# Masked graph attention on one core: the four products of a row tile with rounded weights come first, and the wait for the low weights stands at the two that read them

## The chip, the cores and the metric

The kernel runs on one core of a Trainium2 chip. The metric is the device time of one execution in microseconds (us), and smaller is better. A core has five engines that run their own instruction streams and meet at semaphores: TensorE (PE in the profile; its weight loads are shown apart, as PEld), VectorE (DVE), ScalarE (ACT), GpSimd (POOL) and SyncE (SP, which here only issues DMAs).

## What is computed

With N = 8192 rows and D = 256 columns:

```python
h = jnp.maximum(_layernorm(x, axis=-1), 0.0)
h1 = h @ a[:d]
h2 = h @ a[d:]
e = jax.nn.leaky_relu(h1 + h2.T, negative_slope=0.01)
attention = jnp.where(adj > 0, e, NEG_BIG)
attention = jax.nn.softmax(attention, axis=1)
x = x + attention @ h
```

`adj` is an 8192 x 8192 matrix of int32, 256 MB, so nearly all of the memory traffic is this one matrix.

## The kernel before, in words

The exponential of the leaky sum of two scalars is a maximum of two products, so a weight is `max(r[row], g[col]) * mask` up to factors that depend on the row or on the column alone. The column's factor is put into `h`, and the row's cancels between numerator and denominator. VectorE makes the unnormalised weights with one instruction for each 128 x 512 tile (line 710: `W`).

TensorE multiplies fp32 values in a format with a shorter mantissa. To keep the precision, both factors are split: ScalarE rounds `W` to `w_hi` (line 509), VectorE subtracts to get the rest `w_lo` (line 720), and `h` is kept as `h_hi` and `h_lo` in the same way. A product is then the sum of three: `w_hi` with `h_hi` (line 869), `w_hi` with `h_lo` (line 871) and `w_lo` with `h_hi` (line 872). Columns D and D+1 of `h_hi` carry the split denominator weights.

The matrix is cut into 16 x 16 blocks of 512 x 512. A visit takes a block of 512 rows over some blocks of columns and accumulates in PSUM (`acc`, one bank for each of four row tiles t). There are 24 short visits, of four blocks of columns each, in which `h` of the remaining rows is also made beside the products (phases "whole", "early", "late"), and then eight times a short visit and a long one of twelve blocks of columns (`finals`), after which rows are finished. When a visit ends, ScalarE copies `acc` to SBUF (line 528), GpSimd adds what earlier visits of these rows stored (line 381), and VectorE makes the reciprocal of the denominators (lines 732 to 738) in the middle of its work for the next visit.

A block is worked in two pairs of column tiles (u = 0 and 1). There are 512 pairs in all, numbered g. For a pair TensorE issues 24 matmuls: for each of four row tiles t and for both u, the three products, each with its own weight load. After the first pair of each block it also transposes the mask of a later block (line 831, four instructions; they wait for `mask`, made by ScalarE on line 500, and for `W` of line 710, whose input they replace).

The order around the change is written out by hand. In the loop VectorE does for step g first the rest `w_lo` of pair g-2, then side work, then `W` of pair g. `w_hi` has four buffers (HL = 4), `w_lo` has two (LL = 2), `W` has two. The rest of pair g needs `w_hi` of that pair and waits until TensorE has used pair g-2 (line 719). On TensorE both waits of a pair, for `w_hi` (line 859, semaphore `s_hi`) and for `w_lo` (line 860, semaphore `s_lo`), stand ahead of all of its 24 matmuls. Line 863 waits inside the pair, ahead of each row tile, until the tile's bank has been copied out; it stands in the first pair of a visit only. The signal that a pair is used (line 876) comes from its last matmul.

Of the kernel before, what the change touches and what calls it, by code (L numbers as in the profile page):

```python
# [9 lines left out]
def masked_graph_attention(nc, x, adj, a, out):  # L10
# [4 lines left out]
    ds = bass.ds  # L15

    P = 128
    N, D = x.shape
    G = 4
    BLK = P * G  # L20
# [5 lines left out]
    WC = D + 2  # L26
# [26 lines left out]
    with ctx:  # L53
        def sb(name, shape, dt):
            return ctx.enter_context(nc.sbuf_tensor(name, shape, dt))
# [4 lines left out]
        def sem(name):  # L60
            return ctx.enter_context(nc.semaphore(name))

        h_hi = sb("h_hi", [P, NT, WC], f32r)
# [78 lines left out]
        s_lo = sem("lo_ready")  # L142
# [677 lines left out]
        @block.tensor  # L820
        def _(pe):
            pe.wait_ge(s_const, 1)

            def transpose_mask(n, kc, wait):

                g = n * CI + kc
                pe.wait_ge(s_mask, g + 1)
                if wait:
                    pe.wait_ge(s_w, 2 * (g - 1))
                for t in range(G):  # L830
                    last = nc.tensor.transpose(T[:, kc, t * P:(t + 1) * P], mask_words[:, kc, t, :], ident[:])  # L831
                last.then_inc(s_T, 1)

            def lay_out_first_r():

                pe.wait_ge(s_ex, 1)
                cells = r_first.rearrange("p (q e) -> p e q", e=G)
                for e in range(G):
                    last = nc.tensor.transpose(cells[:, e, :], r_all[:, e:e + 1].to_broadcast([P, P]), ident[:])
                last.then_inc(s_lay, 1)  # L840

            def sum_h(c, parity):

                h = h_bufs[parity]
                pe.wait_ge(s_z, G * (c + 1))
                for e in range(G):
                    last = nc.tensor.matmul(hs_acc, ones[:], h[:, e, :], start=c == 0 and e == 0,
                                            stop=False, skip_group_check=True)
                last.then_inc(s_hsum, 1)

            def add_row_sums():

                pe.wait_ge(s_hs, G * (NB - Q) + 1)
                nc.tensor.matmul(hs_acc, ones[:], hsum[:], start=False, stop=True,
                                 skip_group_check=True).then_inc(s_hm, 1)

            def products(V, c, g, k, start, stop):

                pe.wait_ge(s_hi, g + 1)
                pe.wait_ge(s_lo, g + 1)  # L860
                for t in range(G):
                    if start and not V.head:
                        pe.wait_ge(s_free, G * (V.v - 1) + t + 1)
                    for u in range(2):
                        tile = G * c + 2 * (k % 2) + u
                        cols = slice(u * BLK + t * P, u * BLK + (t + 1) * P)
                        rhs_hi = h_hi[:, ds(tile, 1), :].rearrange("p o w -> p (o w)")
                        rhs_lo = h_lo[:, ds(tile, 1), :].rearrange("p o w -> p (o w)")
                        nc.tensor.matmul(acc[:, t, 0:WC], w_hi[:, k % HL, cols], rhs_hi,  # L869
                                         start=start and u == 0, stop=False)  # L870
                        nc.tensor.matmul(acc[:, t, 0:D], w_hi[:, k % HL, cols], rhs_lo, start=False, stop=False)  # L871
                        last = nc.tensor.matmul(acc[:, t, 0:WC], w_lo[:, k % LL, cols], rhs_hi,  # L872
                                                start=False, stop=stop and u == 1)
                    if stop and t < G - 1:
                        last.then_inc(s_acc, 1)
                last.then_inc(s_used, 1)

            def steps(V, n, c, first, second, last):
                if V.head and first:
                    transpose_mask(0, 0, False)  # L880
                    lay_out_first_r()
                    sum_h(0, 0)
                if first and not V.head and V.its == 2:
                    pe.wait_ge(s_hl, V.c0 + Q)
                for k in range(PI):
                    kc = k // 2
                    m = c + kc
                    if V.head and m == 0 and k == 0:
                        pe.wait_ge(s_l0, 2)
                    elif V.head:  # L890
                        pe.wait_ge(s_hl, m + 1)
                    products(V, c + kc, n * PI + k, k, first and k == 0, last and k == PI - 1)
                    if k % 2 == 0 and V.head:
                        transpose_mask((m + 1) // CI, (m + 1) % CI, m > 0)
                    elif k % 2 == 0 and not (V.tail and last):
                        transpose_mask(n + 1, kc, True)
                    if V.head and k % 2 == 1 and m + 1 < Q:
                        sum_h(m + 1, (m + 1) % CI)
                    if V.head and k % 2 == 1 and m + 1 == Q:
                        transpose_mask(n + 1, 1, True)  # L900
            run(pe, steps, h_made=add_row_sums)
# [23 lines left out]
```

## Time and profile before

| | |
|---|---|
| median of 3 runs | 1642.61 us (1642.26 to 1643.2) |
| time of the profiled execution | 1641.76 us |
| its span | 1640.0 us |
| PE busy | 1600.4 us, 98% |
| PEld busy | 1589.2 us, 97% |
| DVE busy | 1431.7 us, 87% |
| ACT busy | 1182.1 us, 72% |
| POOL busy | 397.8 us, 24% |
| granted TensorE clock | 1.00 of full speed in all but the last stretch |
| DMA | 330.97 MB, 202 GB/s on average |

The busy time of an engine says how full it is, and not what it costs: an engine that is 98% busy sets the time in the stretches in which it never stands still, and in the others something else does. So the page is read for which engine is full, the waits for where the full one stands idle, and the timeline of such a place for what came last.

### The profile page before, as it was taken

The page shows a single profiled execution, that of the slowest core. Times are in us where ns is not written, and L with a number is a line of the kernel's source. Part 1 is how long each engine was busy: PE and PEld are TensorE (multiplying, and loading weights), DVE is VectorE, ACT ScalarE, POOL GpSimd, SP SyncE. Part 2 cuts the span into 40 slices and gives each one's busy share as a digit, 9 for nine tenths or more (in the row PEclk, how much of TensorE's full clock was granted, in tenths as well). Part 3 has the DMA queues.
Part 4 walks back from the last instruction along what each step waited for, and adds up shares of the span by engine and source line. Part 5 has one row for each costly group of instructions (what it writes and reads, how often), then busy time and mean ns, then how long its engine had stood idle before and what let it go on. Part 6 is the DMA issues. An engine that isn't in the chain of part 4 may idle for free.

```text
span 1640.0 us, 38962 instructions
## 1 busy us (share of the span) xinstructions
PE 1600.4 (98%) x13350; PEld 1589.2 (97%) x13350; DVE 1431.7 (87%) x2008; ACT 1182.1 (72%) x1240; POOL 397.8 (24%) x487
## 2 busy tenths in 40 slices
PE   5999999999999999999999999999999999999998
PEld 4999999999999999999999999999999999999998
DVE  7899999999999988888788888888888888888887
ACT  7788778777778766767767767767767766767763
POOL 6344224453344311201201201201301300300400
PEclk9999999999999999999999999999999999999999
DMA  6666767877777777657666656666756756666662
GB/s 206 217 204 217 229 209 223 245 221 245 244 225 232 232 210 229 198 169 206 198 185 194 210 166 191 209 182 176 227 175 184 212 178 189 206 184 183 207 182 74
DMA packets 170376, 330.97 MB, mean 202 GB/s; under 512 B 8640, under 2 KB 26048, under 8 KB 170304
## 3 DMA queue, kind: packets, MB, share of 16 engines
q1 hardware_dynamic: 145248, 288.90, 58.2%
q10 hardware_dynamic: 25056, 41.13, 7.7%
q8 instruction: 43, 0.70, 0.2%
q14 instruction: 29, 0.24, 0.1%
HBM read 308.90 MB, written 21.10 MB: 201 GB/s over the span
## 4 chain that ended last, share of the span: by engine, by line
PE 79%; issue 4%; ACT 4%; POOL 4%; DVE 3%; DMA 2%; ACTq 0%; DVEq 0%; POOLq 0%
PE acc L869 25%; PE acc L872 24%; PE acc L871 24%; PE T L831 6%; POOL stage L381 2%; DMA xo<-part_sums 2%; ACT mask L500 1%; POOL xb L390 1%; DVE W L710 1%; POOL xb L392 1%; ACT hb L564 1%; ACT w_hi L509 1%; ACT stage L563 1%; DVE w_lo L720 1%; ACT stage L528 0%
## 5 line engine op out<-in xcount | busy, mean ns | idle before, releaser
L869 PE MATMUL acc<-h_hi,w_hi 128*128 128x258 f32 (+1 forms) x4096 | 1183.3, 289 | 17.9 <-DVE w_lo L720 14.0
L872 PE MATMUL acc<-h_hi,w_lo 128*128 128x258 f32 (+1 forms) x4096 | 1154.8, 282 | 0.0
L871 PE MATMUL acc<-h_lo,w_hi 128*128 128x256 f32 (+1 forms) x4096 | 1149.4, 281 | 0.0
L509 ACT ACTIVATE w_hi<-W 128x1024 fp32r<-128x1024 f32 x512 | 538.4, 1057 | 359.9 <-DVE W L710 301.1
L869 PEld LDWEIGHTS acc<-h_hi,w_hi 128*128 128x128 f32 x4096 | 772.2, 189 | 24.7 <-ACT w_hi L509 14.4
L710 DVE SCALAR_TENSOR_TENSOR W<-r_rep,g_all,T 128x512 f32<-128x512 f32 (+1 forms) x1024 | 718.4, 743 | 68.7 <-DVE w_lo L720 41.3
L871 PEld LDWEIGHTS acc<-h_lo,w_hi 128*128 128x128 f32 x4096 | 777.3, 190 | 0.0
L872 PEld LDWEIGHTS acc<-h_hi,w_lo 128*128 128x128 f32 x4096 | 773.0, 189 | 0.0
L720 DVE SCALAR_TENSOR_TENSOR w_lo<-W,w_hi 128x1024 fp32r<-128x1024 f32 x512 | 651.7, 1273 | 100.6 <-PE acc L872 71.4
L500 ACT ACTIVATE mask<-adj_in,mhalf 128x2048 fp8e5<-128x2048 int32 x256 | 509.5, 1990 | 26.9 <-POOL xb L392 26.6
L390 POOL TENSOR_TENSOR xb<-xb,stage 128x256 f32<-128x256 f32 x60 | 55.8, 930 | 697.3 <-ACT hb L564 697.3
L831 PE MATMUL T<-ident,mask 128*128 128x128 f32 x1024 | 154.7, 274 | 14.9 <-ACT mask L500 14.2
L381 POOL TENSOR_TENSOR stage<-stage,xo 128x258 f32<-128x258 f32 x96 | 91.6, 985 | 207.5 <-ACT stage L528 207.5
L831 PEld LDWEIGHTS T<-ident,mask 128*128 128x128 f32 x1024 | 118.3, 141 | 18.1 <-issue 14.5
L353 POOL TENSOR_SCALAR hq<-hb,q 128x256 f32<-128x256 f32 x56 | 37.6, 690 | 203.9 <-ACT q L461 173.3
L528 ACT ACTIVATE stage<-acc 128x258 f32<-128x258 f32 x156 | 58.0, 386 | 33.4 <-PE acc L872 31.9
L392 POOL TENSOR_TENSOR xb<-xb,hb 128x256 f32<-128x256 f32 x60 | 63.4, 1057 | 4.7
L370 POOL TENSOR_TENSOR h_lo<-hq,h_hi 128x256 f32 (+1 forms) x60 | 53.3, 919 | 4.6 <-ACT h_hi L480 4.4
L361 POOL TENSOR_TENSOR hsum<-hsum,hb 128x256 f32<-128x256 f32 x48 | 49.5, 1031 | 2.8
L563 ACT ACTIVATE stage<-stage,rinv 128x256 f32<-128x256 f32 x60 | 29.9, 498 | 15.3 <-POOL xb L392 15.3
L699 DVE SCALAR_TENSOR_TENSOR xo<-hb,a_ps 128x256 f32<-128x256 f32 x96 | 36.2, 413 | 1.5 <-issue 0.9
L445 ACT ACTIVATE hb<-xb,shift,rstd 128x256 f32<-128x256 f32 x56 | 30.2, 587 | 1.6 <-POOL shift L318 1.6
(68 smaller groups left out, 221.9 us busy)
## 6 DMA issues: line engine op xcount, KB each, us to landing
adj_in<-in_adj_dram SPq DMA_DIRECT2D x256, 1024.0 KB, 5.4
part_sums<-stage ACTq DMA_DIRECT2D x24, 516.0 KB, 6.5
xo<-part_sums ACTq DMA_DIRECT2D x24, 516.0 KB, 3.6
r_rep<-r_rows SPq DMA_DIRECT2D x39, 256.0 KB, 3.6
xb<-in_x_dram ACTq DMA_DIRECT2D x15, 512.0 KB, 3.9
out_dram<-xb ACTq DMA_DIRECT2D x15, 512.0 KB, 3.2
xb<-in_x_dram SPq DMA_DIRECT2D x14, 512.0 KB, 6.1
xo<-in_x_dram SPq DMA_DIRECT2D x2, 512.0 KB, 5.3
```

The lines of the kernel that those rows point to most:

```text
L381: last = nc.gpsimd.tensor_tensor(stage[:, t, :], stage[:, t, :], prior[:, t, :], ALU.add)
L390: nc.gpsimd.tensor_tensor(xb[:, t, :], xb[:, t, :], stage[:, t, 0:D], ALU.add).then_inc(s_fin, 1)
L392: nc.gpsimd.tensor_tensor(xb[:, t, :], xb[:, t, :], hshare, ALU.add).then_inc(s_o, 1)
L500: nc.scalar.activation(mask8[:, kc, :, :].rearrange("p t j -> p (t j)"), adj_in[:, kc, :, :].rearrange("p t j -> p (t j)"), ACT.Sign, bias ...
L509: nc.scalar.activation(w_hi[:, k % HL, :], W[:, k % 2, :], ACT.Relu).then_inc(s_hi, 1)
L528: nc.scalar.activation(stage[:, t, :], acc[:, t, 0:WC], ACT.Copy).then_inc(s_free, 1)
L710: last = nc.vector.scalar_tensor_tensor(W[:, k % 2, u * BLK:(u + 1) * BLK], r_rep[:, V.v % 2, :], g_all[:, ds(G * c + e, 1)], T8[:, k // 2 ...
L720: nc.vector.scalar_tensor_tensor(w_lo[:, k % LL, :], W[:, k % 2, :], 0.0, w_hi[:, k % HL, :].bitcast(f32), ALU.max, ALU.subtract).then_inc ...
L831: last = nc.tensor.transpose(T[:, kc, t * P:(t + 1) * P], mask_words[:, kc, t, :], ident[:])
L869: nc.tensor.matmul(acc[:, t, 0:WC], w_hi[:, k % HL, cols], rhs_hi, start=start and u == 0, stop=False)
L871: nc.tensor.matmul(acc[:, t, 0:D], w_hi[:, k % HL, cols], rhs_lo, start=False, stop=False)
L872: last = nc.tensor.matmul(acc[:, t, 0:WC], w_lo[:, k % LL, cols], rhs_hi, start=False, stop=stop and u == 1)
```

## The change

Within a row tile t, the inner loop over u is split in two. The first issues lines 869 and 871 for both u (four matmuls, all with `w_hi`), the second issues line 872 for both u (two matmuls with `w_lo`). The wait for `w_lo` moves from the head of the pair to between the two loops of the first row tile. Number, shapes and operands of the matmuls stay as they are, and so do the transposes, the signals and all other engines' instructions. The slice of `h_hi` is written out as its full width.

```diff
             def products(V, c, g, k, start, stop):
 
                 pe.wait_ge(s_hi, g + 1)
-                pe.wait_ge(s_lo, g + 1)
                 for t in range(G):
                     if start and not V.head:
                         pe.wait_ge(s_free, G * (V.v - 1) + t + 1)
                     for u in range(2):
                         tile = G * c + 2 * (k % 2) + u
                         cols = slice(u * BLK + t * P, u * BLK + (t + 1) * P)
-                        rhs_hi = h_hi[:, ds(tile, 1), :].rearrange("p o w -> p (o w)")
+                        rhs_hi = h_hi[:, ds(tile, 1), 0:WC].rearrange("p o w -> p (o w)")
                         rhs_lo = h_lo[:, ds(tile, 1), :].rearrange("p o w -> p (o w)")
                         nc.tensor.matmul(acc[:, t, 0:WC], w_hi[:, k % HL, cols], rhs_hi,
                                          start=start and u == 0, stop=False)
                         nc.tensor.matmul(acc[:, t, 0:D], w_hi[:, k % HL, cols], rhs_lo, start=False, stop=False)
+                    if t == 0:
+                        pe.wait_ge(s_lo, g + 1)
+                    for u in range(2):
+                        tile = G * c + 2 * (k % 2) + u
+                        cols = slice(u * BLK + t * P, u * BLK + (t + 1) * P)
+                        rhs_hi = h_hi[:, ds(tile, 1), 0:WC].rearrange("p o w -> p (o w)")
                         last = nc.tensor.matmul(acc[:, t, 0:WC], w_lo[:, k % LL, cols], rhs_hi,
                                                 start=False, stop=stop and u == 1)
```

## Rows read from the trace of the kernel before

**Rows 1.** The page: busy time, share of the span and instructions of each engine.
```profile
PE 1600.4 (98%) x13350; PEld 1589.2 (97%) x13350; DVE 1431.7 (87%) x2008; ACT 1182.1 (72%) x1240; POOL 397.8 (24%) x487
```
**Rows 2.** TensorE's waits, whole span: waiter and releaser, us in total, times, longest.
```profile
PE T L831 <- ACT mask L500: 14.2, 6, 13.2
PE acc L869 <- DVE w_lo L720: 14.0, 12, 1.6
```
**Rows 3.** TensorE's waits from 650 us to the end.
```profile
PE acc L869 <- DVE w_lo L720: 11.1, 8, 1.4
PE T L831 <- ACT mask L500: 0.9, 5, 0.2
PE T L831 <- DVE W L710: 0.6, 3, 0.2
```
**Rows 4.** TensorE by stretch: bounds, length, busy (matmuls), clock, DMA share, GB/s.
```profile
66.00:154.00 88.00, 87.47 (x708) 1.00 0.69 224
154.00:579.00 425.00, 425.00 (x3587) 1.00 0.75 230
680.00:785.00 105.00, 105.00 (x888) 1.00 0.66 196
805.00:910.00 105.00, 105.00 (x888) 1.00 0.64 195
```
**Rows 5.** VectorE's waits from 60 to 160 us.
```profile
DVE xo L699 <- issue: 0.9, 1, 0.9
DVE W L710 <- DVE w_lo L720: 0.9, 3, 0.3
```
**Rows 6.** Matmuls around the stall at 785 us: start, us, line, idle before and releaser.
```profile
785.16 0.28 PE L872 MATMUL acc<-h_hi,w_lo 128*128 128x258 f32 x1
786.85 0.36 PE L869 MATMUL acc<-h_hi,w_hi 128*128 128x258 f32 x1 [1.41 <-DVE w_lo L720]
787.04 0.28 PE L871 MATMUL acc<-h_lo,w_hi 128*128 128x256 f32 x1
787.16 0.28 PE L872 MATMUL acc<-h_hi,w_lo 128*128 128x258 f32 x1
```
**Rows 7.** ScalarE, timeline of the same stretch.
```profile
779.34 0.39 ACT L528 ACTIVATE stage<-acc 128x258 f32<-128x258 f32 x1 [0.33 <-PE acc L872]
...
781.51 1.05 ACT L509 ACTIVATE w_hi<-W 128x1024 fp32r<-128x1024 f32 x1
...
794.17 1.99 ACT L500 ACTIVATE mask<-adj_in,mhalf 128x2048 fp8e5<-128x2048 int32 x1
```
**Rows 8.** GpSimd and VectorE, timelines of the same stretch.
```profile
779.80 3.55 POOL L381 TENSOR_TENSOR stage<-stage,xo 128x258 f32<-128x258 f32 x4 [7.12 <-ACT stage L528]
...
783.48 0.17 DVE L732 TENSOR_TENSOR dsum<-stage 128x4 f32<-128x4 f32 x1 [2.84 <-POOL stage L381]
...
785.49 1.22 DVE L720 SCALAR_TENSOR_TENSOR w_lo<-W,w_hi 128x1024 fp32r<-128x1024 f32 x1
786.82 1.41 DVE L710 SCALAR_TENSOR_TENSOR W<-r_rep,g_all,T 128x512 f32<-128x512 f32 x2
...
794.75 1.41 DVE L710 SCALAR_TENSOR_TENSOR W<-r_rep,g_all,T 128x512 f32<-128x512 f32 x2
```
**Rows 9.** Matmuls around the short stall ten microseconds later.
```profile
795.82 0.28 PE L872 MATMUL acc<-h_hi,w_lo 128*128 128x258 f32 x1
796.29 0.65 PE L831 MATMUL T<-ident,mask 128*128 128x128 f32 x4 [0.19 <-DVE W L710]
```
**Rows 10.** First pair of a visit: matmuls with a wait inside the pair (line 863).
```profile
777.94 0.28 PE L872 MATMUL acc<-h_hi,w_lo 128*128 128x258 f32 x1
778.05 0.29 PE L869 MATMUL acc<-h_hi,w_hi 128*128 128x258 f32 x1
778.18 0.28 PE L871 MATMUL acc<-h_lo,w_hi 128*128 128x256 f32 x1
```
**Rows 11.** One line each: register instructions of TensorE's sequencer at lines 869 and 871.
```profile
L869 PEldq FUSED_REGOPS  x320: 60/60/79, 679.4 to 1617.3; - x160
L871 PEldq FUSED_REGOPS  x320: 46/46/51, 679.5 to 1617.5; - x160
```

## The prediction

> **What bounds the kernel now.** I read the page first. TensorE is busy for 98% of the span and VectorE for 87% [rows 1], so the question is where TensorE stands idle and who ends it. The waits of TensorE answer that: 14.2 us go to the first mask (one wait of 13.2 us at the start, which the change doesn't touch), and 14.0 us in 12 waits to line 720, the low weights [rows 2]. That second row is what the change aims at, and its 14.0 us, 0.9% of the time, are the most that it could ever give by this wait. Next I read where these waits lie. 11.1 us of the 14.0 are eight waits after 650 us, of up to 1.4 us [rows 3]: one in each of the eight repeats of `finals`. Last, the table by stretch: from 154 to 579 us, from 680 to 785 and from 805 to 910 TensorE is busy for the whole stretch [rows 4], so there the time is the number of matmuls times their spacing, and no wait counts. From 66 to 154 us it is not quite full (87.47 of 88.00). VectorE, in the same time, waits for nobody but ScalarE once and itself [rows 5]: there VectorE is the bound, and TensorE runs dry by a little at many pairs.
>
> So three kinds of place matter: the stretch to 154 us where VectorE sets the pace, the long full stretches, and the eight stalls.
>
> **The wait, where it moves.** While `w_lo` is late, TensorE may now do four matmuls with `w_hi` instead of none. Matmuls start 0.12 us apart (787.04 and 787.16 in [rows 6]), or 105 us / 888 = 0.118 us in a full stretch, transposes included [rows 4]. Four are 4 x 0.12 = 0.48 us. The wait stands in the first row tile, so this is all that can be brought forward, however long the stall: the other 20 matmuls stay behind it. For it to happen `w_hi` must be there. At the stall of 785 us the last matmul of the pair ahead starts at 785.16, and the next only at 786.85, when line 720 (785.49 + 1.22 = 786.71) has ended [rows 6, 8]. The `w_hi` of that pair was written from 781.51 to 782.56 [rows 7], over two microseconds before the stall, so the four can go at once. The stall of 1.41 us becomes about 0.9 us, in the middle of the pair.
>
> Eight such stalls would be 8 x 0.48 = 3.8 us. I take none of it, for what comes next is late too. After 783.48 VectorE works without a pause [rows 8]: its chain starts with the denominators, which wait for GpSimd's additions, which wait for the copy of line 528, which waits for the end of the visit on TensorE [rows 7, 8]. Nothing in this chain waits for the pairs that TensorE does after 785. Ten microseconds later TensorE ends a pair (last start 795.82) and stands again, until the transposes start at 796.29 [rows 9]. Two inputs end together there: the mask, 794.17 + 1.99 = 796.16 [rows 7], and `W`, 794.75 + 1.41 = 796.16 [rows 8]. Both hang on the chains of ScalarE and VectorE, not on TensorE. A TensorE that is 0.48 us ahead arrives at 795.34 instead of 795.82 and waits 0.48 us longer for the same moment. The gain of the first wait is given back in full at the second. [rows 3] show the second kind in all eight repeats (5 and 3 waits). So the finals count 0.
>
> In the stretch that ends at 154 us there is no such second gate: TensorE's only waits there are for line 720, and behind it TensorE is full for 425 us [rows 4]. A stretch in which VectorE sets the pace does not get shorter by TensorE's head start, as each later wait absorbs the one before. But TensorE leaves it 4 x 0.12 = 0.48 us ahead, once, and carries that to the end: the copy of line 528 and all that hangs on it start from TensorE's last matmul of a visit [rows 7], so the eight repeats move ahead as a whole. Term: -0.5 us.
>
> **The wait as an instruction.** 512 waits now stand inside a pair. A wait that is already met may cost something where it breaks a run of matmuls. The nearest row is line 863, also a wait inside a pair, ahead of the row tiles t = 0 to 3 of a visit's first pair: starts 777.94, 778.05, 778.18, spaced as everywhere [rows 10]. From this row a met wait costs 0 (bound below: a gain is excluded, as there is nothing to save in a full stretch). The bound above is a full restart as after a stall: the second matmul follows the first by 0.19 us instead of 0.12 [rows 6], 0.07 x 512 = 36 us. I take 0. The rule that speaks against this is in the Trainium skill, TensorE: Matmul & The Clock Gate, section "Part 2: What happens when you issue a matmul": weight loads are pulled ahead of matmuls in flight, through a window of 64 instructions. If a wait closed that window, every pair would pay for one weight load that nothing hides, and the sum would be the restart's price; the spacing of line 863's pair says that it does not.
>
> **The order of the matmuls.** Same number, same shapes, same bank for six in a row. In each row tile two of six neighbourhoods are new (line 871 followed by 869, and 872 followed by 872), 2 x 4 x 512 = 4096 in all. The trace of before has neither. The nearest rows give starts that differ by 0.11 to 0.13 us from one matmul to the next [rows 10], which is mostly rounding; from 888 and 888 matmuls in two full stretches of 105 us the mean repeats exactly [rows 4]. I take 0 for it and bound it by 1 ns either way, 4096 x 0.001 = 4 us: an estimate, from the fact that two stretches agree to less than one matmul in 888 while single rows show 10 ns.
>
> **The sum.** The profiled execution took 1641.76 us, 1.76 us more than its span of 1640.0. The sum against it is 1641.76 - 0.5 = 1641.3. The median of the runs is 0.85 us above the profiled one, so the median of the changed kernel is 1642.6 - 0.5 = 1642.1 us.
>
> **The rivals.** *The finals keep their gain.* If the transposes' gate moved with TensorE, each of eight stalls would keep 0.48 us: 1642.6 - 0.5 - 3.8 = 1638.3 us. For it speaks only that both gates end at the same moment, and so could both depend on something that moves; against it the unbroken chain of VectorE from 783.48 on [rows 8].
>
> *The waits inside the pairs are not free.* This is the slower case: a met wait keeps the next weight load from starting ahead. It would show in all 512 pairs, costs 0.07 us in each, and decides from 0.007 us a pair on (3.3 us). 1642.1 + 36 = 1678 us. Against it are [rows 10]. By the window of the Trainium skill (TensorE: Matmul & The Clock Gate, "Part 2: What happens when you issue a matmul") a closed window would be this case.
>
> *The new order runs at another spacing.* By the bound above 1638 to 1646 us, each way alike; for it speaks that nothing in the trace shows the new neighbours.
>
> *The change does nothing of what it says.* If `w_hi` came as late as `w_lo`, or the lead at 154 us were lost at the first mask behind it, 1642.6 us. The weight loads' `w_hi` at 781.51 [rows 7] speaks against the first.
>
> **How the numbers follow.** The forecast, 1642.1 us, has a chance of 0.60; nothing at all (1642.6) 0.10; the finals keep their gain 0.08; a spacing that moves the time by over 3 us 0.12, evenly to both sides; a spacing that moves it by less 0.06; waits or register instructions that cost 0.04. A measurement of this kernel can tell 0.2%, 3.3 us, from no change. Faster by more: 0.08 + 0.06 = 0.14. Slower by more: 0.06 + 0.04 = 0.10. The rest, 0.76, is within. The range reaches from the finals' rival, 1638.0, to the spacing's upper bound, 1646.0; left out are the 36 and 16 us cases and the ends of the spacing.
>
> **What the profile of the changed kernel would show.** TensorE's waits for line 720 should stand at line 872 and not at 869, and sum to 14.0 - 12 x 0.48 = 8 us or a little more. Its waits ahead of line 831 should grow by about as much as those shrink after 650 us, 8 x 0.48 = 3.8 us; that pair of numbers is the heart of the argument. The stretch from 680 to 785 us should hold 888 matmuls again, give or take one: 880 would mean that waits, register instructions or the order cost 1%. The prediction is wrong if the row of line 831 has not grown (then the finals kept their gain), or if a full stretch has another count.

## The result, and the profile after

| | before | changed |
|---|---|---|
| median, same chip | 1641.93 us (21 runs) | 1645.06 us (1644.65 to 1645.81, 21 runs) |
| ratio | | 1.0019, 95% interval 1.0013 to 1.0025 |
| profiled execution, span | 1641.76, 1640.0 us | 1645.0, 1643.2 us |

The changed kernel is 3.1 us slower. That is clear of its interval, and with 0.19% it lies just below the 0.2% (3.3 us) that the prediction took as the least that can be told. The forecast of 0.5 us less has the wrong sign.

One slip in the text ahead of the prediction: the long visits of `finals` cover all sixteen blocks of columns, not twelve. Nothing in the sum used it.

Line 869 of before is 868 in the changed kernel, 871 is 870, 872 is 877. First TensorE's waits from 650 us on (waiter and releaser, us in total, times, longest), to be held against [rows 3]:

```profile
PE acc L877 <- DVE w_lo L720: 5.9, 8, 0.8
PE T L831 <- DVE W L710: 2.5, 6, 0.4
PE T L831 <- ACT mask L500: 0.9, 2, 0.4
```

The wait for the low weights has moved to the line that reads them and fell from 11.1 to 5.9 us. What stands ahead of the transposes grew from 1.5 to 3.4 us. Now TensorE by stretch (bounds, length, busy with the number of matmuls, clock, DMA share, GB/s), the same stretches as [rows 4]:

```profile
66.00:154.00 88.00, 87.18 (x713) 1.00 0.69 224
154.00:579.00 425.00, 425.00 (x3572) 1.00 0.75 228
680.00:785.00 105.00, 105.00 (x885) 1.00 0.65 195
805.00:910.00 105.00, 105.00 (x885) 1.00 0.63 191
```

Here is the loss. In 425 us in which TensorE never stands still it starts 3572 matmuls instead of 3587, and 885 instead of 888 in each of the two 105 us stretches. 425 us / 3587 = 118.5 ns and 425 / 3572 = 119.0 ns: half a nanosecond more a matmul there, at the same granted clock of 1.00. By the prediction's own sign (888, give or take one) this already says that something in it is wrong. Last, the stall that [rows 6] show in the kernel before, as it is now (start, us, line):

```profile
787.47 0.28 PE L870 MATMUL acc<-h_lo,w_hi 128*128 128x256 f32 x1
788.51 0.51 PE L877 MATMUL acc<-h_hi,w_lo 128*128 128x258 f32 x2 [0.76 <-DVE w_lo L720]
788.86 0.28 PE L868 MATMUL acc<-h_hi,w_hi 128*128 128x258 f32 x1
```

The four products with rounded weights are done when it begins, and the idle time is 0.76 instead of 1.41 us.

Sorting the starts of all matmuls of the trace by what stands between two of them gives the account of the last 319 pairs (from 632 us in the kernel before to the end). It is worked out from the traces, start to start, in us, with counts in brackets. A step ahead of the transposes counts as a stall from 0.3 us on. Steps among the transposes and back to the products have no row of their own, so the rows don't add up to the total. The last two columns belong to runs e4 and e8 below.

```
                              before        changed        e4            e8
product to product       873.90 (7324) 876.35 (7324) 874.40 (7321) 875.38 (7322)
 second after a gap       33.63 (166)   33.84 (166)   35.21 (177)   35.09 (176)
 with a stall, w_lo       13.31 (8)      8.13 (8)      0.00          0.00
to transposes, no stall   18.80 (147)   18.34 (140)   18.25 (140)   19.70 (152)
to transposes, stall       4.67 (11)     8.91 (18)    16.62 (18)     2.55 (6)
total                   1001.25       1003.02       1001.89        989.67
```

The stalls for `w_lo` gave 5.2 us. Ahead of the transposes 4.2 us more are lost in stalls, or 3.8 us if both rows are taken together, since seven crossings passed the limit of 0.3 us. The step from one product to the next took 2.5 us, and the rest (second matmuls after a gap, steps at the transposes) 0.7 us. So these pairs took 1.8 us longer, and the other 1.4 us of the loss came before them. Which row is behind the slower kernel, and why steps got longer, is what the experiments are for.

### The profile page after: what moved, and what is told of

The parts are those of the page before. It is cut to its first block, busy times and chain, and to the rows that moved or that the text cites. A ratio compares the mean times of both kernels' runs of the same rounds, so it can differ in the third digit from the quotient of the medians.

```text
span 1643.2 us, 38460 instructions
## 1 busy us (share of the span) xinstructions
PE 1605.5 (98%) x13350; PEld 1593.7 (97%) x13350; DVE 1431.8 (87%) x2008; ACT 1182.7 (72%) x1240; POOL 396.9 (24%) x487
## 4 chain that ended last, share of the span: by engine, by line
PE 74%; DVE 7%; issue 6%; POOL 4%; ACT 3%; DMA 2%; ACTq 0%; DVEq 0%; POOLq 0%
PE acc L877 23%; PE acc L868 23%; PE acc L870 23%; PE T L831 5%; DVE w_lo L720 3%; DVE W L710 3%; POOL stage L381 2%; DMA xo<-part_sums 2%; POOL xb L392 1%; POOL xb L390 1%; ACT mask L500 1%; ACT hb L564 1%; ACT w_hi L509 1%; ACT stage L563 1%; ACT stage L528 0%
## 5 line engine op out<-in xcount | busy, mean ns | idle before, releaser
L868 PE MATMUL acc<-h_hi,w_hi 128*128 128x258 f32 (+1 forms) x4096 | 1091.3, 288 | 6.6 <-POOL h_hi L372 3.1
L870 PE MATMUL acc<-h_lo,w_hi 128*128 128x256 f32 (+1 forms) x4096 | 1065.3, 281 | 0.0
L877 PE MATMUL acc<-h_hi,w_lo 128*128 128x258 f32 (+1 forms) x4096 | 829.7, 284 | 7.3 <-DVE w_lo L720 7.2
L877 PEld LDWEIGHTS acc<-h_hi,w_lo 128*128 128x128 f32 x4096 | 626.6, 188 | 10.4 <-DVE w_lo L720 10.2
```

## Experiments

Two theories at the start: (A) the order of the matmuls costs, since in the new order the steps between them are longer; (B) the waits inside the pairs cost, which the prediction had as its slower rival. Each half of the change was run alone. "Ratio" is always against the kernel before on the same chip, with its 95% interval.

**e1_order_alone.** The changed kernel with both waits at the head:

```diff
                 pe.wait_ge(s_hi, g + 1)
+                pe.wait_ge(s_lo, g + 1)
...
-                    if t == 0:
-                        pe.wait_ge(s_lo, g + 1)
```

> New order of the matmuls, both waits at the head of the pair. The changed kernel took 3.1 us more than before. Theory A, the order: matmuls of the new order start 0.3 ns further apart on average (3572 in the full 425 us from 154 us on, where before has 3587), so this kernel costs as much as the changed one, +3 to +4 us against before (ratio 1.002), and the full stretch of 425 us holds some 3572. Theory B, the waits inside the pairs cost: 512 x 0.007 us are gone here, ratio 1.000, and the stretch holds 3587.

Measured: 1646.37 us, ratio 1.0022 (1.0012 to 1.0032).

**e2_wait_alone.** The kernel before with the wait between line 871 and line 872 of the first row tile:

```diff
                 pe.wait_ge(s_hi, g + 1)
-                pe.wait_ge(s_lo, g + 1)
...
                         nc.tensor.matmul(acc[:, t, 0:D], w_hi[:, k % HL, cols], rhs_lo, start=False, stop=False)
+                        if t == 0 and u == 0:
+                            pe.wait_ge(s_lo, g + 1)
```

> Old order of the matmuls, the wait for the low weights moved from the head to ahead of the first line that reads them, so two matmuls earlier than that wait. Theory A, the order costs and the moved wait does not: ratio 1.000, the full stretch holds 3587, time lower than before by the 2 x 0.12 = 0.24 us that TensorE leaves the stretch to 154 us earlier. The eight stalls of `finals` shrink by 0.24 us each at the low weights and grow by as much ahead of the transposes. Theory B, a wait inside a pair costs: +3 us, 1.002.

Measured: 1642.12 us, ratio 0.9998 (0.9989 to 1.0007). The full stretch of 425 us, e1 first, then e2:

```profile
154.00:579.00 425.00, 425.00 (x3571) 1.00 0.75 229
```
```profile
154.00:579.00 425.00, 425.00 (x3586) 1.00 0.75 230
```

3571 with the new order, 3586 with the old one and the moved wait: theory A holds and B falls. 512 waits inside pairs cost nothing that shows, as line 863's pair had said [rows 10]. The moved wait isn't even an instruction of its own any more: where both waits stand at the head (before, e1), the weight-load sequencer has 510 wait instructions of 51 ns at line 860, and in the changed kernel and e2 it has 8, at line 859.

A comparison pair by pair leaves out the start of the execution, which differs by a microsecond or two from trace to trace. From the start of pair 48 to that of the last pair, worked out from the traces, the changed kernel took 3.66 us more than before, e1 3.69 us more, and e2 0.26 us less. With the new order it makes no difference behind pair 48 whether the wait was moved.

**e3_grouped_order.** Both waits at the head, and one more order: the two products of `w_hi` with `h_hi`, the two with `h_lo`, the two with `w_lo`.

```diff
                         nc.tensor.matmul(acc[:, t, 0:WC], w_hi[:, k % HL, cols], rhs_hi,
                                          start=start and u == 0, stop=False)
+                    for u in range(2):
+                        ...
                         nc.tensor.matmul(acc[:, t, 0:D], w_hi[:, k % HL, cols], rhs_lo, start=False, stop=False)
```

> Third order within a row tile, both waits at the head: both products of rounded weights with rounded h, then both with the rest of h, then both with low weights. If the spacing of matmuls depends on which follows which, this has a spacing of its own, between 0.997 and 1.004 of before, and none of the mechanisms that I have says which. If it is the wait that costs (theory B), this has the ratio 1.000.

Measured: 1646.62 us, ratio 1.0022 (1.0013 to 1.0031), 3577 matmuls in the stretch. A third order has a spacing of its own too, here also a longer one.

**e4_all_hi_first.** This one tests the other half of the prediction, the gate at the transposes. A second loop over the row tiles holds the low products, so all 16 others come ahead of the wait (against the changed kernel):

```diff
-                    if t == 0:
-                        pe.wait_ge(s_lo, g + 1)
+                pe.wait_ge(s_lo, g + 1)
+                for t in range(G):
                     for u in range(2):
...
                         last = nc.tensor.matmul(acc[:, t, 0:WC], w_lo[:, k % LL, cols], rhs_hi,
                                                 start=False, stop=stop and u == 1)
```

> All 16 products with rounded weights of a pair first, then the wait, then the 8 with low weights: 16 x 0.12 = 1.9 us can be brought forward, so the stalls for low weights (1.4 us each) vanish. Theory A, the gate at the transposes ten microseconds later takes back what a stall gives: TensorE's idle time ahead of line 831 after 650 us grows from 4.7 (before) and 8.9 (changed) to some 14 us over the eight repeats, and the time is that of the changed kernel less 1 to 1.5 us (head start at 154 us) and plus or minus the spacing of this order. Rival: the gate moves along, and 8 x 1.4 = 11 us less than before remain.

Measured: 1645.92 us, ratio 1.0022 (1.0013 to 1.0031). Its waits from 650 us on:

```profile
PE T L831 <- ACT mask L500: 9.4, 11, 1.1
PE T L831 <- DVE W L710: 2.1, 5, 0.4
```

No wait for line 720 is left (11.1 us before, [rows 3]), and the waits ahead of line 831 have gone from 1.5 to 11.5 us. The account above says the same from the starts: 13.3 us less at `w_lo`, 12.0 us more in stalls at the transposes (11.4 with both rows). The gate does not move along, and it takes back nearly all of it. What else e4 lost, it lost earlier: at pair 193 it is 2.2 us behind the kernel before, and its stretch of 425 us holds 3567 matmuls instead of 3587.

If that is so, then reaching the gate later must free what the stalls give. **e6_late_transposes** takes the kernel before, order and waits untouched, and issues the transposes inside the next pair:

```diff
-                    elif k % 2 == 0 and not (V.tail and last):
-                        transpose_mask(n + 1, kc, True)
...
+                    if midway is not None and t == 1:
+                        midway()
```

Here `midway` is the same call, handed to `products` of the odd pair; the first visit keeps its order. **e7_all_hi_late_8** and **e8_all_hi_late_16** put it after the 8th and the 16th matmul of a pair in e4.

> The kernel before with its order and both waits at the head, but the four transposes of the mask (line 831) stand after the second row tile of the next pair instead of ahead of it, 12 x 0.12 = 1.4 us later (outside the first visit). Theory: the gate at 796 us is reached later than the mask is ready, so the idle time ahead of the transposes in the eight repeats (0.47 us in 0.12 each at 795 and 0.3 at 802, some 3.2 us beyond a normal step in all) goes, if VectorE, which gets its transposed mask 1.4 us later, keeps its lead: -2 to -3 us, 1640. Rival: VectorE now waits for the transposes and TensorE for VectorE: slower, +2 us or more.

> All 16 products with rounded weights first, then the wait, then the 8 with low weights, and the transposes after the 8th matmul of the next pair, 0.95 us later than before. In the run with all 16 first the stalls for low weights were gone (13.3 us to 0) and those ahead of the transposes had grown from 4.7 to 16.6 us. Theory of the gate: each of some two gates a repeat gets 0.95 us shorter, so that 8 x 0.95 to 8 x 1.9 us return: 1631 to 1638 us. Rival: the next wait behind this gate (VectorE's or ScalarE's) takes its place, 1645.

> As the run before, with the transposes after the 16th matmul of the next pair, 1.9 us later than before. Theory of the gate: nearly all of the 16.6 us ahead of the transposes goes, 1630 to 1634 us. Rival: VectorE needs the transposed mask by then, its weights come late in every block, and TensorE waits for rounded weights: slower than 1645 us.

Measured: e6 1637.53 us, ratio 0.9969 (0.9957 to 0.9981); e7 1638.24 us, 0.9973 (0.9963 to 0.9984); e8 1633.47 us, 0.9948 (0.9934 to 0.9961). TensorE's waits from 650 us on, e6 and then e8:

```profile
PE acc L869 <- DVE w_lo L720: 11.0, 8, 1.4
```
```profile
PE T L831 <- ACT mask L500: 0.2, 1, 0.2
```

In e6 only the stalls for `w_lo` are left, in e8 as good as nothing. e6 gained 4.8 us, more than the 2 to 3 expected. In its last 319 pairs the steps ahead of the transposes take 4.2 us less than before and those among the transposes 0.8 us less; the expectation had put the first at 3.2 us and had not thought of the second. e8's last 319 pairs took 11.6 us less than before, but it came to them 2.8 us late. e7's expected range of 1631 to 1638 was missed by little: its gates still hold 4.7 us. The rival of e6 and e8 was that VectorE, which gets its transposed masks later, would now be late itself. VectorE does wait, e6 from 154 us to the end:

```profile
DVE W L710 <- PE T L831: 82.6, 145, 0.8
```

TensorE waits for none of it. But these 82.6 us are for the most part no new idle time: VectorE's waits for TensorE at line 719 (for a used pair) fell from 71.4 to 6.9 us, and those of line 710 for its own line 720 from 40.4 to 24.4. All its waits from 154 us on sum to 159.9 us before and 162.6 us in e6. In e8 they sum to 192.8 us, 33 us more than before, and there too TensorE waits for none of it.

**What makes a step long.** Mean steps start to start, from one product of a pair to the next, in ns, given at the first of the two. They are worked out from all pairs but the first 32, without the first two steps of a pair and without steps of 200 ns or more. H and L are the two halves, weight first, and the digit is u, so HL1 is `w_hi` with `h_lo` of the odd tile.

```
before    HH0 119.1 HL0 118.6 LH0 118.5 HH1 122.2 HL1 117.7 LH1 119.8   mean 119.34
e2        HH0 119.0 HL0 118.6 LH0 118.6 HH1 122.1 HL1 117.7 LH1 119.8   mean 119.33
changed   HH0 119.5 HL0 119.8 HH1 120.6 HL1 117.4 LH0 119.7 LH1 121.7   mean 119.69
e1        HH0 119.5 HL0 119.7 HH1 120.6 HL1 117.3 LH0 119.7 LH1 121.6   mean 119.68
```

These means repeat to 0.1 ns from one kernel to another with the same order, which is why half a nanosecond can be trusted. The longest is behind a matmul that reads an odd tile of `h_hi`. A row of such a tile has 258 x 4 = 1032 bytes, so odd tiles start 8 bytes behind a multiple of 16. Two ways to change that (both also move the buffers behind `h_hi`, by 32 bytes in e5 and by 512 in e9 and e10 in the built programs, and no run separates the two effects):

**e5_shift_h_hi** moves all of `h_hi` up by 8 bytes (a small buffer shares memory to make room), so that even tiles stand where odd ones stood:

```diff
-        h_hi = sb("h_hi", [P, NT, WC], f32r)
+        h_hi_mem = sb("h_hi", [P, NT * WC + 2], f32r)
+        h_hi = h_hi_mem[:, 2:NT * WC + 2].rearrange("p (n w) -> p n w", w=WC)
...
-        half = sb("half", [P, 2], f32)
...
+        half = den[:, 0:2]
```

> The kernel before, with all tiles of rounded h 8 bytes higher in SBUF (a row of such a tile has 258 x 4 = 1032 bytes, so even tiles start at a multiple of 16 bytes and odd tiles 8 behind one; the shift swaps them). In the kernel before, the start after a matmul that reads an odd tile comes 122 or 120 ns later, after an even tile 119, after a tile of the rest of h 118. If that is the start address, the long steps move to the even tiles, and the mean stays within 0.2 ns: ratio 1.000. If it is the place in the order, nothing moves.

Measured: 1639.37 us, ratio 0.9983 (0.9974 to 0.9992). The long steps moved over (HH0 121.3, HH1 118.7, LH0 120.0, LH1 118.5), as the theory of the start address wants. That the mean also fell, to 119.04, and the time with it (a ratio of 1.000 was expected), can come from the buffers that moved along.

The start modulo 16 is not all that a step depends on. Sorted further, by the pair's number modulo 4 (from pair 48 on), LH1 in the kernel before goes from 118.5 to 121.2 ns, and e2 repeats this (118.5 to 121.1). The table's means hide it.

**e9_aligned_old_order** and **e10_aligned_new_order** space the tiles by 260 elements in either order (to make room, the identity matrix stands in for the matrix of ones; the column sums come out wrong, and the work is the same); **e11_shift_new_order** is the changed kernel with the shift.

```diff
-        h_hi = sb("h_hi", [P, NT, WC], f32r)
+        h_hi_mem = sb("h_hi", [P, NT, WC + 2], f32r)
+        h_hi = h_hi_mem[:, :, 0:WC]
...
-        ones = sb("ones", [P, P], f32)
+        ones = ident
...
-            nc.gpsimd.memset(ones[:], 1.0)
```

> The kernel before with the tiles of rounded h 260 elements apart instead of 258, so that all start at a multiple of 16 bytes. To make room the identity matrix stands in for the matrix of ones, so the column sums of h, which count only for rows without neighbours, are not computed rightly; the work is the same. After an 8-byte shift the long steps went with the tiles that start 8 bytes behind a multiple of 16 (even ones 121 ns, odd ones 119). Theory, start address: the mean step within a pair falls from 119.3 ns to that of aligned tiles, some 118.5, in 12288 matmuls -10 us: about 1632 us, ratio 0.994. Rival (the shift helped by the relation to other buffers, not by alignment): 1639 to 1642.

> The changed kernel with the same spacing of 260 elements (and the same stand-in for the ones). If the order costs only through which matmul the unaligned tiles meet, this and the kernel with the old order now have the same mean step, within 0.1 ns, and the same time within 1 us. If the new order has a cost of its own, the difference of 0.35 ns a matmul, 3 to 4 us, stays.

> The changed kernel with the 8-byte shift of all tiles of rounded h. The shift gave the old order 3 us (0.9983) and moved its long steps from odd to even tiles. If the new order loses only by where the unaligned tiles stand in it, swapping even and odd should move it also, by 2 us or more either way. If the order costs by itself: 1645.0 - 3 = 1642 us, 3 us behind the shifted old order.

Measured: e9 1639.60 us, 0.9982 (0.9973 to 0.9991), mean step 118.78 ns. e10 1640.61 us, 0.9989 (0.9980 to 0.9998), 119.01 ns. e11 1642.16 us, 0.9997 (0.9988 to 1.0006), 119.42 ns. Alignment is worth 3.1 us to the old order and not the 10 that I had worked out from the even tiles' steps: HH1 is still at 120.5 ns with every tile aligned, so the start modulo 16 is a part of the long steps and not all of it; by the pair's number modulo 4, HL1 of e9 goes from 114.1 to 119.6 ns with every tile aligned. Between the two orders 1.0 us is left with aligned tiles (their intervals overlap), and 2.4 us with shifted ones, each held against the kernel before on its own chip (these intervals overlap too). By the mean step the orders are 0.23 ns apart with aligned tiles and 0.38 with shifted ones, against 0.35 without either. So the cost of the new order seems to shrink when no tile is unaligned, but swapping even and odd doesn't cure it.

**Neighbourhoods.** e13 and e14 change one pair of neighbours each in the new order, e15 and e16 take two columns from the low products (their share of the denominators is left out), in the old and the new order:

```diff
 e13, low products
-                    for u in range(2):
+                    for u in (1, 0):
...
-                                                start=False, stop=stop and u == 1)
+                                                start=False, stop=stop and u == 0)
```
```diff
 e15 and e16
-                        last = nc.tensor.matmul(acc[:, t, 0:WC], w_lo[:, k % LL, cols], rhs_hi,
+                        last = nc.tensor.matmul(acc[:, t, 0:D], w_lo[:, k % LL, cols], rhs_hi[:, 0:D],
```

In e14 the four products of the first loop run HH0, HL0, HL1, HH1.

> The changed kernel with the two low products of a row tile in the other order (u = 1 ahead of u = 0). In the changed kernel the step after the low product of the odd tile, ahead of the next row tile, is 121.7 ns, the one between the two low products 119.7, the one into them 117.4. If the long step belongs to the unaligned tile that is read second of two, the low product of the odd tile now comes first of the three with 258 columns and its step falls to 119 to 120: mean step 119.3 to 119.5 instead of 119.7, 1641 to 1643 us. If the order costs otherwise: 1645, as the changed kernel.

> The changed kernel with the products of the odd tile in the other order (rest of h ahead of rounded h), so that runs of 258 columns are four long (rounded h of the odd tile, two low products, rounded h of the next row tile). If runs of 258 columns cost, this is slower than the changed kernel by 1 us or more, 1646 us. If the position of the odd tile counts alone: about the changed kernel, 1645.

> The kernel before with 256 columns instead of 258 in the low products: their share of the denominators is left out. 4096 x 2 columns less; at the full clock 2 columns are 0.8 ns, so 3.4 us less than before if the step follows the columns, 1639. Beside the next run it serves as the reference for its order.

> The changed kernel with 256 columns in the low products (their share of the denominators left out). No two matmuls with 258 columns stand together any more. If runs of 258 columns are what the new order costs, this is as fast as the old order with 256 columns, within 1 us. If not, it stays 3 us behind it.

| | time, us | ratio | mean step, ns |
|---|---|---|---|
| e13 | 1639.88 | 0.9984 (0.9975 to 0.9993) | 119.24 |
| e14 | 1643.62 | 1.0007 (0.9998 to 1.0016) | 119.43 |
| e15, old order, 256 | 1637.93 | 0.9971 (0.9959 to 0.9982) | 118.83 |
| e16, new order, 256 | 1638.42 | 0.9973 (0.9963 to 0.9984) | 118.98 |

e13 differs from the changed kernel in nothing but which low product comes first. It is 2.7 us faster than the kernel before on its chip where the changed kernel was 3.1 us slower, so the swap gave 5 to 6 us. Its full stretch:

```profile
154.00:579.00 425.00, 425.00 (x3589) 1.00 0.75 230
```

The two low products now take 120.8 (odd) and 118.2 ns, where they took 119.7 (even) and 121.7: the long step shrank but stayed with the odd tile, while HH1 fell by 0.9 and HL0 by 0.8 and HH0 behind them rose by 0.9. With 256 columns in the low products the orders are 0.5 us apart instead of 3.1, within their intervals (0.15 ns by the mean step). e15 came 4.7 us below the kernel before, where 3.4 were expected from the two columns alone. A plain rule "long runs of 258 columns cost" finds no support in e14: it has the longest runs, its mean step is shorter than the changed kernel's, and its time is some 2 us nearer to before (its interval ends at 1.0016, the changed kernel's starts at 1.0013). So the cost of an order varies with both, the placement of the tiles and the columns of neighbours, and no rule of mine forecasts it. **Open**: the mechanism. The runs rule out the moved wait as a cause. They show that the order, the placement of the buffers and the column count each can move the mean step by some tenths of a nanosecond (up to 0.45, 0.67 and 0.7); they don't show what inside TensorE or its reads makes the step.

**e12_shift_all_hi_late_16** puts the two finds together, e8 with the 8-byte shift:

> All 16 products with rounded weights first, transposes after the 16th matmul of the next pair (1633.5 us without the shift), with the 8-byte shift. If the shift works as on the kernel before, -2 to -3 us more: 1630 to 1632. If it works on the neighbourhoods of the old order only: 1633 to 1634.

Measured: 1632.18 us, ratio 0.9936 (0.9923 to 0.9950), the lowest time of all the runs, 10.5 us below the kernel before on that chip. Held against the kernel before on either chip, the shift gave 1.6 us here (2.0 by the ratios); the intervals of e8 and e12 overlap, so it is not told from the 2 to 3 us expected, nor from nothing.

## Why the prediction was right or wrong

**The step that failed** is "The order of the matmuls", where I took 0 with a bound of 4 us either way. It measured +3 to +4 us: 0.35 ns on the mean step, +3.8 us in e1 (0.0022 x 1642.55 = 3.6 by the ratio), and +3.7 us from pair 48 on in both kernels with the new order. The size is inside the bound; the value taken was wrong, and with a term of -0.5 us beside it this alone turned the sign. The reason given was bad too. That two stretches of before agree to a matmul in 888 says that the spacing of one order repeats. It says nothing about another order. The count of new neighbourhoods was short as well: by line two of six are new, but by tile, which the runs show to matter, `w_hi` with `h_lo` of the odd tile is now followed by the low product of the even one, and that makes three. The trace of before did hold a warning that I read as rounding: at full resolution its mean steps are 117.7 to 122.2 ns by position, and e2 has the same ones. If one position costs 4 ns more than another, thousands of new neighbours may cost several microseconds, of either sign. The rival with this cause had a chance of 0.06 on the slow side above 3 us (and 0.06 below); nearer 0.2 each way would have been honest.

**The gate in the finals: right.** The prediction's pair of numbers was a wait for `w_lo` that shrinks after 650 us and one ahead of the transposes that grows, by 3.8 us each. By the account from starts the stalls shrank by 5.2 us and the steps ahead of the transposes grew by 3.8 us in all. Of the 5.2 us, four products in each of eight stalls are 4.0 us, which is the prediction's 3.8. Another 0.7 us is a quicker restart that the prediction didn't have: with the wait alone at its matmul TensorE starts 0.055 us after line 720 ends, and with both waits at the head 0.145 us after it. The remaining 0.4 us is that TensorE comes to the place later by its longer steps, and the weights a little earlier. By the waits that the profile names, the shrinkage is 5.2 and the growth 1.9 us, as these count idle time from the modelled end of a matmul; the account from starts is the better one. Changed kernel and e1 differ only in the wait, by 4.8 us in these stalls, and from pair 48 on not at all in the time: the finals count 0. e4 confirms it with a larger lever and e8 from the other side. The rival "the finals keep their gain" is refuted.

**The head start of 0.48 us: not resolved.** Pair 48 starts at 184.6 us in before and 184.2 in the changed kernel, 0.4 less. But e2, with 0.24 us forecast, reaches pair 48 0.1 us later than before, and e1, with nothing forecast, 1.0 us later, so the start scatters by more than the term. In the time e2 was 0.4 us less than before within an interval of 1.5 us either way. No run here can tell the term from nothing.

**A wait inside a pair: right**, 0, by e2 (3586 matmuls against 3587). The Trainium skill (TensorE: Matmul & The Clock Gate, "Part 2: What happens when you issue a matmul") says that weight loads are pulled ahead of matmuls in flight. The rival was that a wait inside a pair ends this. In e2's trace a met wait doesn't, by the count of matmuls.

**Register instructions: right.** Line 868 still has 320 of them, and line 877 none, so the split loop found the registers of the first.

**A reading.** The prediction says by [rows 5] that VectorE waits for ScalarE once. Those rows don't show ScalarE; the profile has it there with 0.6 us in three waits. Nothing in the sum used it.

**The range** held the time (1638.0 to 1646.0), as it took the order's bound in; the forecast's sign was wrong.

## What to carry to other kernels

When an engine is full, a reordering of its own instructions is never free by argument: compare how many it starts in a full stretch, and try both neighbours of each kind, for here a swap of two equal products was worth 5 to 6 us of 1640. When a stall is to be shortened, look for the next wait behind it that doesn't hang on this engine: what the first gives, the second takes, until the gate is reached later too (e8: -9 us, where shortening the stall alone gave nothing). And where an engine with room to spare gets its input later, its waits cost nothing as long as nobody waits for it (e8: VectorE waits 33 us more in sum); look at the sum before calling a wait new, as it may have moved from another line (e6: 82.6 us at one line, 2.7 us more in sum).

## What the runs showed of the hardware

The mean step of an fp32 matmul with 256 or 258 columns, each with its own weight load, is 117 to 122 ns by position at a granted clock of 1.00. It varies with where the operands lie: with `h_hi` shifted by 8 bytes, steps behind tiles that now start 8 bytes behind a multiple of 16 grew and the others shrank (e5: HH0 from 119.1 to 121.3, LH0 from 118.5 to 120.0, HH1 from 122.2 to 118.7, LH1 from 119.8 to 118.5). The steps behind `h_lo`, whose tiles kept their start modulo 16, moved too (HL0 from 118.6 to 117.0, HL1 from 117.7 to 118.7), so the start of the tile read is not the whole of it. The Trainium skill (TensorE: Matmul & The Clock Gate, "Back-to-back issue gap") gives N / 2.4 + 2.5 ns for an isolated matmul, which is 110 ns for 258 columns, and for a stream with weight loads 81 ns at 128 columns and 131 ns at 512. In these traces the steps are 7 to 12 ns above the first, and spread by 4 ns at the same count. The same mean step comes back to 0.02 ns in two kernels with the same order (before and e2, changed and e1), so differences of 0.1% can be read from a trace where the times of runs need dozens of them.

A wait that is alone at its matmul restarts TensorE 0.055 us after the instruction that it waits for (changed kernel, e2), and two waits at one place 0.145 us after it (before, e1); the second wait is then a sequencer instruction of 51 ns.
